# Row pairs and guard steps of the first pairs of query tiles at other chunks, in an attention kernel on one Trainium2 core

## What is computed

```python
def _L0_attn_ref(hidden_states, Wq, bq, Wk, bk, Wv, bv, Wo, bo, rel_k, rel_v):
    idx = jnp.clip(pos[None, :] - pos[:, None], -MAX_REL, MAX_REL) + MAX_REL
    rk2 = rel_k[idx]
    rv2 = rel_v[idx]
    attn1 = jnp.einsum('bhqd,bhkd->bhqk', q, k)
    attn2 = jnp.einsum('bhqd,qkd->bhqk', q, rk2)
    attn = jax.nn.softmax((attn1 + attn2) / scale, axis=-1)
    w1 = jnp.einsum('bhqk,bhkd->bhqd', attn, v)
    w2 = jnp.einsum('bhqk,qkd->bhqd', attn, rv2)
    x = (w1 + w2).transpose(0, 2, 1, 3).reshape(B, S, E)
    out = x @ Wo.T + bo
    return out
...
x = x + _L0_attn_ref(_layernorm(x, axis=-1), ...)
x = x + _L0_ffn_ref(_layernorm(x, axis=-1), ...)
```

## Time and profile before

| | |
|---|---|
| median of 3 timed runs | 1291.97 us (1291.25 to 1292.47) |
| profiled execution, its time | 1285.89 us |
| its span, first to last instruction | 1284.2 us |
| mean granted TensorE clock | 0.977 |
| busy: PE / PEld | 1211.6 us (94%) / 838.5 us (65%) |
| busy: DVE / ACT / POOL | 916.4 (71%) / 735.9 (57%) / 576.4 us (45%) |
| DMA queue q1, share of 16 engines | 19.0% |

### The profile page before, as it was taken

One profiled execution on the slowest core, in us unless ns is written; L12 is line 12 of the kernel. 1 busy time (PEld: TensorE's weight loads), 2 busy tenths in 40 slices (PEclk: granted clock), 3 DMA queues, 4 the chain that ended last, 5 costly groups with the idle time before them and its releaser, 6 DMA issues. The chain is left out here.

```text
span 1284.2 us, 60118 instructions
## 1 busy us (share of the span) xinstructions
PE 1211.6 (94%) x26968; PEld 838.5 (65%) x26976; DVE 916.4 (71%) x1751; ACT 735.9 (57%) x1382; POOL 576.4 (45%) x1079
## 2 busy tenths in 40 slices
PE   4788589999999999999999999999999999999998
PEld 3555256676667666666766667677666667767675
DVE  5887777777777777777777777777777776156664
ACT  5787156665666666666666666666666666623332
POOL 5986434453544444544434354544444544022221
PEclk9999579999999999999999999999999999999999
DMA  4576200201111110202020211111110200022321
GB/s 142 185 238 217 66 24 20 59 24 54 37 42 46 32 56 27 63 15 68 10 69 28 59 32 55 46 40 54 36 53 26 69 9 9 8 71 83 90 75 50
DMA packets 101000, 76.51 MB, mean 60 GB/s; under 512 B 12744, under 2 KB 96520, under 8 KB 100744
## 3 DMA queue, kind: packets, MB, share of 16 engines
q1 hardware_dynamic: 100744, 72.67, 19.0%
HBM read 44.86 MB, written 26.21 MB: 55 GB/s over the span
## 5 line engine op out<-in xcount | busy, mean ns | idle before, releaser
L1166 DVE TENSOR_REDUCE b_mx<-b_a 128x1 f32<-128x512 f32 x1024 | 657.7, 685 | 201.2 <-PE b_a L845 197.7
L1111 ACT ACTIVATE b_p<-b_s 128x512 f32<-128x512 f32 x1024 | 569.6, 595 | 379.9 <-PE b_s L904 238.8
L801 POOL TENSOR_TENSOR qd<-q,one 48x512 bf16<-48x512 bf16 x256 | 266.2, 1040 | 479.6 <-PE b_s L904 461.6
L960 PE MATMUL b_pv<-b_p,vg 128*32 128x256 f32 x4096 | 277.0, 384 | 0.2 <-ACT b_p L1111 0.2
L904 PE MATMUL b_s<-qd,z 112*128 112x32 bf16 (+1 forms) x6016 | 248.4, 188 | 0.6 <-issue 0.6
L845 PE MATMUL b_a<-k,q 48*128 48x512 bf16 x1024 | 204.6, 395 | 22.0 <-DVE b_mx L1166 13.2
L904 PEld LDWEIGHTS b_s<-qd,z 112*128 112x128 bf16 (+1 forms) x6016 | 204.6, 98 | 10.6 <-issue 0.7
L866 PE MATMUL b_s<-q,k 54*128 54x64 bf16 (+5 forms) x4096 | 187.6, 206 | 2.7 <-DMA q<-b_mt 1.2
L866 PEld LDWEIGHTS b_s<-q,k 54*128 54x128 bf16 (+1 forms) x4096 | 112.5, 95 | 96.9 <-PE b_s L866 29.5
L960 PEld LDWEIGHTS b_pv<-b_p,vg 128*32 128x32 f32 x4096 | 117.9, 109 | 64.8 <-issue 20.6
L845 PEld LDWEIGHTS b_a<-k,q 48*128 48x128 bf16 x1024 | 51.5, 94 | 87.3 <-ACT b_p L1111 25.9
(11 more groups left out here) (144 smaller groups left out, 1224.6 us busy)
## 6 DMA issues: line engine op xcount, KB each, us to landing
x<-in_x SPq DMA_DIRECT2D x24, 256.0 KB, 3.3
scratch_qop<-a_parts SPq DMA_DIRECT2D x16, 384.0 KB, 2.5
scratch_kop<-a_parts SPq DMA_DIRECT2D x16, 384.0 KB, 3.1
k<-scratch_kop SPq DMA_DIRECT2D x32, 192.0 KB
q<-scratch_qop SPq DMA_DIRECT2D x32, 192.0 KB
scratch_v<-a_vr SPq DMA_DIRECT2D x16, 256.0 KB, 3.2
k<-scratch_kop SPq DMA_DIRECT2D x32, 128.0 KB
q<-scratch_qop SPq DMA_DIRECT2D x32, 128.0 KB
```

Of the source, the lines that this page charges most:

```text
L801: nc.gpsimd.tensor_tensor(dst, src, one, ALU.mult).then_inc(s["qd_ready"], 1)
L960: nc.tensor.matmul(PV[V32 * a:V32 * (a + 1), g * PT:(g + 1) * PT], v[:, side, half, t, 2 * a + g, :], PR[pos][:, 4 * a + 2 * half + g, :], ...
L1111: nc.scalar.activation(out, src, ACT.Exp, scale=SCALE).then_inc(s["p_ready"], 1)
L1166: nc.vector.tensor_reduce(MX[unit.v % 2][:, h:h + 1], PA[(HP * n + hp) % NBANK][:, :], AX_X, ALU.max, negate=True).then_inc(s["a_used"], 1)
```

## The change

A tuple `EXTRA` of chunk numbers takes the place of `AHEAD`. Chunks are counted through, 16 to a pair. In the chunks named in it, 0, 1, 12 and 14 of pair 0 and 4 and 12 of pair 1, there are two row pairs, in all others one, so the lead of 18 is reached in chunk 12 of pair 1 and not in chunk 5 of pair 0. On TensorE the second row pair of such a chunk now stands behind the chunk's scores; VectorE takes the reductions in the same order of numbers as before. The guard steps of unit 1 go from chunk 3 to 4, of unit 2 from chunk 10 to 13 (SyncE's from 11 to 14), of unit 3 from chunk 1 to 3 of pair 1. The relative values of unit 1 go from chunks 12, 13 and 14 (one part each) to chunk 14 (two parts) and 15 (one), and VectorE's masking of them from 14 to 15. Pair 2 and all later ones are as they were. Line numbers of the changed kernel are 7 to 10 higher than those of before.

```diff
--- before.py
+++ after.py
@@ -50,8 +50,8 @@
 PT = 2 * P
 CHUNKS = 16
 PB2 = 2 * CHUNKS
-AHEAD = 18
 FIRST = 12
+EXTRA = (0, 1, 12, 14, CHUNKS + 4, CHUNKS + 12)
 QB = 2
 QROW = 64
 QROWS = QROW * (QB - 1) + OPR
@@ -673,15 +673,22 @@
     def pairs_beside(pair, c):
         n = CHUNKS * pair + c
-        extra = AHEAD - FIRST
-        first = n + FIRST + min(n, extra)
-        return [r for r in range(first, first + (2 if n < extra else 1)) if r < HH * U]
+        first = n + FIRST + sum(e < n for e in EXTRA)
+        return [r for r in range(first, first + 1 + (n in EXTRA)) if r < HH * U]
     def blocks(t, i, g):
         half = P // QB // 2
         near = {0: range(half * g, half * (g + 1)), -1: range(REL // QB), 1: range((P - REL) // QB, P // QB)}
         return near[t - i]
+
+    def second_guard(pair):
+
+        return (4, 3)[pair] if pair < 2 else 1
+
+    def first_guard(pair):
+
+        return 10 if pair else 13
     def freed(n):
@@ -728,11 +735,11 @@
                     if ahead and c == NLOAD:
                         sp.wait_ge(s["s_ready"], PB2 * pair + 2 * c + 1)
                         load_values(sp, k, d, batch + 1, (batch + 1) % 2)
-                    if c == (1 if pair else 3):
+                    if c == second_guard(pair):
                         guard_rows(Unit(2 * pair + 1))
                     if c == 10 and pair:
                         store(pair - 1)
-                    if c == 11 and pair < LAST:
+                    if c == first_guard(pair) + 1 and pair < LAST:
                         guard_rows(Unit(2 * pair + 2))
                 if pair == 8:
                     for p in range(2):
@@ -847,7 +854,7 @@
             def row_pairs_ahead(pair, c):
-                for n in pairs_beside(pair, c):
+                for n in pairs_beside(pair, c)[:1]:
                     row_pair(n)
             def bank(pair, c, n):
@@ -1055,7 +1062,9 @@
                 first, second = Unit(2 * pair), Unit(2 * pair + 1)
                 for c in range(CHUNKS):
                     scores(pair, c)
-                    if c == (1 if pair else 3):
+                    for n in pairs_beside(pair, c)[1:]:
+                        row_pair(n)
+                    if c == second_guard(pair):
                         guard_transpose(second)
                     if pair and c in (2, 3):
                         value_products(pair - 1, 3, range(2 * (c - 2), 2 * (c - 1)))
@@ -1065,15 +1074,17 @@
                         relative_values(first, (4, 6, 7).index(c))
                     if pair and c == 9:
                         output_transposes(pair - 1)
-                    if c == 10:
-                        if pair < LAST:
-                            guard_transpose(Unit(2 * pair + 2))
+                    if c == first_guard(pair) and pair < LAST:
+                        guard_transpose(Unit(2 * pair + 2))
                     if c in (10, 11):
                         value_products(pair, 0, range(2 * (c - 10), 2 * (c - 9)))
                     if c >= 12:
                         value_products(pair, 1 + (c - 12) // 2, range(2 * (c % 2), 2 * (c % 2) + 2))
-                    if c in (12, 13, 14):
+                    if pair and c in (12, 13, 14):
                         relative_values(second, c - 12)
+                    if pair == 0 and c in (14, 15):
+                        for part in ((0, 1), (2,))[c - 14]:
+                            relative_values(second, part)
                     if pair == LAST:
                         if c == 1:
                             first_attention_transposes(0)
@@ -1136,11 +1147,11 @@
             for pair in range(PAIRS):
                 for c in range(CHUNKS):
                     exponentials(pair, c)
-                    if c == (1 if pair else 3):
+                    if c == second_guard(pair):
                         guard_copy(Unit(2 * pair + 1))
                     if pair and c == 7:
                         output_copy(pair - 1)
-                    if c == 10 and pair < LAST:
+                    if c == first_guard(pair) and pair < LAST:
                         guard_copy(Unit(2 * pair + 2))
                     if pair == LAST:
                         if c == 1:
@@ -1215,7 +1226,7 @@
                         keep_values(Unit(2 * pair))
                     if c == 9 and pair:
                         normalise(pair - 1)
-                    if c == 14:
+                    if c == (14 if pair else 15):
                         keep_values(Unit(2 * pair + 1))
                     if pair == LAST:
                         if c == 3:
```

## The result

| | before | changed |
|---|---|---|
| median of 20 timed runs each | 1290.7 us | 1295.57 us |
| lowest and highest | 1285.89, 1292.56 | 1290.25, 1298.27 |
| profiled execution, span | 1285.89, 1284.2 us | 1291.6, 1289.9 us |

The ratio is 1.0037, with a 95% interval of 1.0026 to 1.0048: the changed kernel is 4.8 us slower, between 3.4 and 6.2. The forecast was 1295.6 us, 3.6 us slower than before. The direction and the size of the difference hold; that the time itself came out within 0.1 us is in part luck, as said further down.

The account below looks back on a forecast made before the run. TensorE's own time was taken as the bound from chunk 6 of pair 0, a DMA landing before it. 0 + 3.4 + 0.2 = +3.6 us on 1291.97 gave 1295.6 us; 8-in-10 range 1290.8 to 1297.0.

Parts of the forecast that it names:

- The front is covered by the DMA: Chunks 0 to 5 of pair 0: 4.4 us won on TensorE goes into waiting for unit 1's guard rows; gain 0.
- Four late row pairs: Chunks 12, 14 of pair 0 and 4, 12 of pair 1: 0.63 wait plus 0.22 work each, 3.4 us.
- the 0.1 us in each chunk 13: Both chunks 13: the next row pair finds VectorE still some 0.1 us behind, 0.2 us together.
- The new wait in chunk 4: Chunk 4 of pair 0: first relative-value step waits 1.4 us more, for ScalarE's copy of unit 1's guard transpose.
- The moved guard steps: Units 2 and 3's guard steps and unit 1's relative values moved later: no TensorE wait, counted as 0.
- The late rise: TensorE's clock rises one chunk pair later than before: +1.2 us more, 1296.8 us; chance 0.06.
- a: Guard rows of unit 1 not held by the backlog, chunk 6 starts 4.3 us earlier: 1291.3 us; chance 0.12.
- b: Chunk 6 4.3 us earlier and late row pairs cost only TensorE's 0.22 us each: 1288.6 us; chance 0.12.
- c: The backlog holds but the late row pairs' waits do not show: +0.9 us, 1292.9 us; chance 0.13.
- early d: TensorE's clock rises before chunk 6 and stays, four chunks gain 2.4 us: +1.2, 1293.2 us; chance 0.07.

Follow-up runs that it names:

- split_loads: Changed kernel with six of batch 1's twelve q and k loads, and the values, issued behind unit 1's guard rows: 1290.16 us, ratio 0.9994.
- lead16_split: Changed kernel without pair 1's late row pairs, guard steps, relative values, masking as before, half of batch 1's loads behind unit 1's guard rows: 1285.54 us.
- guards_back: Changed kernel with guard steps, relative values and VectorE's masking back at the chunks of before: 1295.34 us, ratio 1.0033.
- front_six: Changed kernel with all six second row pairs in chunks 0 to 5 of pair 0, behind the scores: 1289.99 us, ratio 0.9986.
- half_reduce: Changed kernel with the four reductions that the late row pairs wait for taken over 256 of 512 columns: 1292.90 us, ratio 1.0018.
- ahead: Changed kernel with the four late second row pairs straight behind the first ones, ahead of the scores: 1294.71 us, ratio 1.0045.
- front_four: Changed kernel with second row pairs only in chunks 0 to 3, guard steps, relative values and masking as before: 1289.40 us, ratio 0.9988.
- front_four_split: front_four with half of batch 1's loads issued behind unit 1's guard rows: 1283.91 us, ratio 0.9960.

## Why the prediction was right

- **The front is covered by the DMA.** Right. Predicted gain at chunk 6: 0; measured 1.0 in the one profiled execution. The executions with unsplit loads scatter from 20.9 to 22.2 us between chunk 0 and 6, with vg's issue, whatever stands in the front, so the 1.0 can't be told from 0. The row that carried it was vg's 7.2 us. split_loads shows the cause by taking it away: 3.8 us. The Trainium skill (DMA: Bandwidth & Descriptors, Queues, rings and completion order) leaves the order of completion between engines open; here the guard rows did not overtake the loads in any execution with all of these ahead.
- **Four late row pairs.** Predicted 3.4 + 0.2, measured 3.66. The wait was right: without it the row pair would have started at 182.71, it started at 183.34, 0.63 us later. Two small terms were off and cancelled. TensorE's own part of a row pair was read ahead of L866 (0.22); ahead of the value products it is 0.32 (183.34 to 183.66). And the 0.1 us in each chunk 13 did not come, because chunk 12 of pair 0 lasted 2.50 us (182.16 to 184.66) and not 2.28. Each late row pair costs 0.95, and chunk 1 of pair 1, which the guard step left, is 0.14 shorter.
- **The new wait in chunk 4.** Predicted 1.4 us (0.56 to 1.97 after the scores), measured 1.96 (159.52 to 161.48). It costs nothing as long as the DMA covers it; with the loads split, lead16_split, where it is gone, starts chunk 6 1.5 us earlier than split_loads.
- **The moved guard steps.** Counted as 0; guards_back and front_six show it. No wait appeared at chunk 0 or 6 of pair 1.
- **The clock.** The late rise, given 0.06, took place in the profiled execution of the changed kernel and cost 1.46 us there. It can't be put down to the change: front_six and half_reduce have it too, ahead, with the same front, and guards_back do not. Which of the timed runs had it can't be read from what is on record.
- **The size.** 4.8 us measured against 3.6, inside the interval's 3.4 to 6.2. Whether the 1.2 us are anything was not settled; a late rise of the clock in a part of the runs would be of that size. The time was met by luck: the forecast started from 1291.97 us, the median of three runs, where that of 20 is 1290.7, and the 1.3 us that its start was too high cancel the 1.2 us that its sum was too low.
- **The rivals.** None of the signs against the forecast came up: chunk 6 began at 168.13 and not before 166 (a and b), the four waits are there (b and c), and the clock was 0.50 until 180.6 (early d).

## What to carry to other kernels

A run of waits on one engine is worth only what the last of them is worth: before thinning out work ahead of a join, look at what ends the wait at the join. A transfer of 12 KB took 5.0 to 7.2 us here from issue to release, and not 2.9, when loads of the next batch stood ahead of it on the queue; issuing half of them after it made the same schedule 3.8 us shorter. And work moved from a stretch where the engine waits to one where it is the bound pays its full time, plus a wait if it comes sooner than the buffer ahead of it is free.

## What the runs showed of the hardware

The granted clock does not follow the front alone. In the kernel before it had fallen to 0.50 at 129.5, ahead of the first row pair, and stayed there for 47.8 us; in the changed kernel it stayed for 51.2 us, until 180.6. Over all twelve profiled executions this low stretch lasted 44.4 us in two (front_four and front_four_split), 47.8 in seven and 51.2 in three, and with one front it came out at 51.2 (changed kernel, half_reduce) and at 47.8 (ahead). In lead16_split (chunk 6 at 169.20) TensorE's busy time by stretch is

```profile
169.00:174.00 5.00, 4.80 (x105) 3.45 (x106) 3.31 (x6) 2.72 (x6) 2.04 (x2) 0.50 0.50 101
174.00:179.00 5.00, 5.00 (x116) 4.26 (x113) 2.65 (x5) 2.39 (x4) 1.08 (x6) 0.50 0.41 115
179.00:184.00 5.00, 4.81 (x83) 2.57 (x76) 2.58 (x4) 2.04 (x5) 1.41 (x4) 0.55 0.06 18
```

without a break from 169.20 to 179.6, where a gap of 0.19 us stands, and again after it, and yet the clock is 0.50 until about 183.5 (0.55 on the mean of 179 to 184). In the kernel before it rose 8.3 us after the wait ahead of chunk 6, here 14.3 us after chunk 6 began. Counted from chunk 0 the two are alike, 30.1 and 29.8 us. In front_four, where chunk 6 starts at 170.75, the stretch 170 to 180 has

```profile
170.00:180.00 10.00, 9.25 (x237) 7.23 (x241) 6.32 (x11) 4.74 (x9) 1.73 (x8) 0.73 0.02 4
```

so the clock rose within 5 us of it, at about 175.4 and 26.6 us after chunk 0. In lead16_split the early chunk 6 is at the half clock for longer, and the kernel gives back 2.5 us of its 6.3 between chunks 6 and 12 (14.82 against 12.36). The Trainium skill (TensorE: Matmul & The Clock Gate, Part 1) has activity releasing the throttle; lead16_split shows that TensorE busy without a break was not enough for it in those 10 us. What sets the moment stays open; the prediction's sentence that it rose with TensorE busy since 169.05 described it and did not explain it.

Executions of one kernel differ by 6 us and more, which is most of the spread in the tables. In the profiled executions chunk 0 of pair 0 starts between 147.3 and 154.1 us, in code that no kernel here touches. In guards_back, the latest, the projection stage has in the stretch 80 to 90

```profile
80.00:90.00 10.00, 8.65 (x38) 5.09 (x39) 7.89 (x22) 4.94 (x9) 4.94 (x7) 0.75 0.39 134
```

against, in the changed kernel,

```profile
80.00:90.00 10.00, 8.97 (x54) 6.15 (x55) 9.38 (x26) 8.61 (x18) 9.10 (x12) 1.00 0.82 262
```

and one wait of TensorE on VectorE of 5.0 us, where the changed kernel has 2.5 at the same place:

```profile
PE a_pq L350 <- DVE a_gd L585: 5.0, 1, 5.0
```

These 2.5 us and the lower clock are a part of the 6.7 us by which its chunk 0 is later; what sets them off was not looked into. So stretches were compared from chunk 0 on, and the whole time only over many runs.
